# Building three of four blocks of gated one-hot rows for the first four groups inside the experts' stage

## The reference, cut to what matters

```
N, T, D = (4, 512, 128); NUM_EXPERTS = 8; k = int(EXPERT_CAP * t / NUM_EXPERTS)
probs = softmax(einsum('ntd,de->nte', x, gate_w)); probs = transpose(probs, (0, 2, 1))
g, m = top_k(probs, k)                              # gains and chosen tokens
xin = vmap(lambda xb, mb: xb[mb])(x, m)
h = gelu(einsum('nekd,edf->nekf', xin, w1)); h = einsum('nekf,efd->nekd', h, w2)
weighted = g[..., None] * h
out = zeros((n * t, d)).at[flat_idx].add(weighted)  # flat_idx: the chosen tokens
x = x + layernorm(out as bfloat16)
```

## Time and profile before

| | us |
|---|---|
| Median of 3 runs | 3795.21 |
| Lowest and highest run | 3792.87, 3801.27 |
| The profiled execution's own time | 3797.36 |
| Its span, first to last instruction | 3795.6 |
| Its mean granted TensorE clock | 0.868 |
| TensorE busy | 2975.8 (78%) |
| VectorE busy | 2390.8 (63%) |
| ScalarE busy | 1816.6 (48%) |
| GpSimd busy | 516.4 (14%) |

### The profile page before, as it was taken

The page is one execution under the profiler, slowest core; times in us unless marked ns, Lnnn a source line. Parts: engine busy times, 40 slices in busy tenths (PEclk is TensorE's granted clock), DMA queues, the critical chain, the costliest instruction groups (busy, mean ns, idle before and its releaser), DMA issues.

```text
span 3795.6 us, 76097 instructions
## 1 busy us (share of the span) xinstructions
PE 2975.8 (78%) x31950; PEld 2354.3 (62%) x31950; DVE 2390.8 (63%) x6446; ACT 1816.6 (48%) x3876; POOL 516.4 (14%) x643
## 2 busy tenths in 40 slices
PE   6788887778888758778884887967778798686885
PEld 3466665456666547667774765856666486574564
DVE  4655555565554578888897666467565845755337
ACT  3556555555555467777773443324434332343222
POOL 1110001120100132222222011120010202002000
PEclk7889988888998879898997988987989899697887
DMA  2000000000000010000000000000000000001000
GB/s 86 1 1 1 1 1 1 1 1 1 1 1 1 1 51 6 7 9 6 7 1 12 2 2 1 2 1 2 2 1 3 1 2 1 1 3 45 1 1 23
DMA packets 13542, 27.99 MB, mean 7 GB/s; under 512 B 784, under 2 KB 9232, under 8 KB 12688
## 3 DMA queue, kind: packets, MB, share of 16 engines
q1 hardware_dynamic: 13200, 23.12, 1.8%
HBM read 21.02 MB, written 2.10 MB: 6 GB/s over the span
## 4 chain that ended last, share of the span: by engine, by line
PE 50%; DVE 36%; ACT 10%; issue 3%; POOL 1%; DMA 0%; SPq 0%; DVEq 0%; POOLq 0%; ACTq 0%
PE ps L331 6%; DVE LN L1944 5%; PE ps L322 4%; PE ps L1822 3%; PE ps L1303 3%; DVE RS L237 3%; PE ps L388 3%; PE ps L296 3%; PE ps L475 3%; DVE M L491 2%; DVE LN L1957 2%; ACT LN L268 2%; PE ps L1314 2%; DVE LN L258 2%; PE ps L1766 1%
## 5 line engine op out<-in xcount | busy, mean ns | idle before, releaser
L304 ACT COPY LN<-ps 128x512 f32<-128x512 f32 (+4 forms) x592 | 303.3, 546 | 629.4 <-PE ps L296 172.2
L283 POOL TENSOR_TENSOR RS<-RS,MISC 128x4 f32<-128x4 f32 x216 | 219.2, 1015 | 2177.2 <-DVE RS L249 1642.6
L296 PE MATMUL ps<-cons,LN 128*128 128x128 f32 x672 | 143.2, 356 | 349.7 <-DVE LN L256 124.8
L296 PEld LDWEIGHTS ps<-cons,LN 128*128 128x128 f32 x672 | 97.8, 178 | 403.7 <-DVE LN L256 143.9
L491 DVE TENSOR_REDUCE M<-ps 128x6 f32<-128x768 f32 x256 | 242.0, 955 | 140.1 <-PE ps L475 95.7
L1944 DVE TENSOR_TENSOR LN<-LN 128x1024 f32<-128x1024 f32 (+2 forms) x192 | 220.3, 1147 | 27.8 <-ACT LN L304 16.9
L388 PE MATMUL ps<-LN 32*128 32x256 f32 x1024 | 187.4, 440 | 53.3 <-DVE LN L527 32.1
L632 DVE TENSOR_REDUCE M<-ps 128x12 f32<-128x1536 f32 x64 | 112.4, 1756 | 175.2 <-PE ps L378 175.2
L322 PE MATMUL ps<-LN,wAB 128*128 128x512 f32 x384 | 207.1, 672 | 14.3 <-ACT LN L341 8.5
L1822 PE MATMUL ps<-LN,wAB 128*128 128x128 f32 x1024 | 150.9, 310 | 74.3 <-ACT LN L304 73.8
L391 PE MATMUL ps<-LN 32*128 32x256 f32 x1024 | 202.9, 475 | 0.8 <-DVE M L491 0.8
(11 more groups left out here) (345 smaller groups left out, 7563.3 us busy)
## 6 DMA issues: line engine op xcount, KB each, us to landing
wAB<-wb SPq DMA_DIRECT2D x16, 256.0 KB, 2.7
LN<-wd SPq DMA_DIRECT2D x8, 512.0 KB, 6.9
wAB<-wa SPq DMA_DIRECT2D x1, 3840.0 KB, 16.1
wCs<-wc SPq DMA_DIRECT2D x1, 2336.0 KB, 10.7
XA<-xin SPq DMA_DIRECT2D x8, 256.0 KB, 7.6
y<-XA SPq DMA_DIRECT2D x8, 256.0 KB, 2.3
wAB<-wb SPq DMA_DIRECT2D x1, 1024.0 KB, 5.0
wAB<-wm SPq DMA_DIRECT2D x1, 1024.0 KB, 4.8
```

The lines of the kernel that those rows point to most:

```text
L283: pool.e.tensor_tensor(c.r[:, 40:44], c.r[:, 36:40], mhalf, ALU.pow).then_inc(*c.G.inc((k, "rstd")))
L296: ins = pe.e.transpose(ps[:, n * 128:(n + 1) * 128], src[:, n, :], ident)
L304: act.e.copy(dst, ps).then_inc(*c.A.inc(named(k, done)))
```

## The change

The eight instructions of a block, with their waits, become a function `dve_gated`. `dve_expert` calls it for the blocks (0, 0), (0, 1) and (1, 1) of the lane's first group: each ahead of the copy of one of the lane's first three items. `dve_put` then builds for the first four groups only block (1, 0). For groups 4 to 7 it builds all four as before. So that three blocks of a group can exist at once, block (1, 1) of group q < 4 lies in the token tiles of group q + 4; block (1, 0) still shares a buffer with (0, 0) and waits for its transposes. A block built in the experts' stage waits for the take stage of all sixteen sequences.

```diff
+        def gated_rows(q, m):
+            z = q + 4 if m and q < 4 else q
+            return [LN[:, 30720 + 512 * (q % 4):31232 + 512 * (q % 4)], LN[:, 16384 + 512 * z:16896 + 512 * z]]
...
             for it in range(n, 16, 4):
                 ex, hf = it // 2, it % 2
                 yield
+                if it < 12:
+                    dve_gated(dve, c, n, *((0, 0), (0, 1), (1, 1))[it // 4])
                 yield
                 dve_copy(dve, c, ("ex", it), YS[:, ex, 4 * hf:4 * hf + 4, :], v4(c.ps[0]), "sum", "y")
                 yield
+
+        def dve_gated(dve, c, q, m, eh):
+            if q < 4 and (m, eh) != (1, 0):
+                for b in range(16):
+                    dve.wait_ge(PD[b % 4], (("take", b), "taken", 1))
+            elif q < 4:
+                dve.wait_ge(c.P, (("put", q), 0, 0, "og_tr"))
+            elif m == 0:
+                dve.wait_ge(c.P, (("put", q - 4), 1, eh, "og_tr"))
+            else:
+                dve.wait_ge(c.P, (("put", q), 0, eh, "og_tr"))
+            g4 = gated_rows(q, m)[eh].rearrange("p (e b s) -> p e b s", e=4, b=2)
+            for e_ in range(4):
+                for b2 in range(2):
+                    cc = 8 * (2 * q + b2) + 4 * eh + e_
+                    ins = dve.e.tensor_scalar(g4[:, e_, b2, :], iota, RK[:, m, cc:cc + 1], GM[:, m, cc:cc + 1],
+                                              ALU.is_equal, ALU.mult)
+            ins.then_inc(*c.D.inc((("put", q), m, eh, "og")))
...
                 for m in range(2):
                     for eh in range(2):
-                        if m:
-                            dve.wait_ge(c.P, (k, 0, eh, "og_tr"))
...
-                        ins.then_inc(*c.D.inc((k, m, eh, "og")))
+                        if q >= 4 or (m, eh) == (1, 0):
+                            dve_gated(dve, c, q, m, eh)
                         yield
```

More of the change, by code:

```diff
@@ L2164, in pe_put @@
                 k = ("put", q)
-                og = [LN[:, 30720 + 512 * n:31232 + 512 * n], LN[:, 16384 + 512 * q:16896 + 512 * q]]
                 for m in range(2):
+                    og = gated_rows(q, m)
                     for eh in range(2):
```

## The result

The change takes 3775.43 us (median of 6 runs, 3769.0 to 3778.56) against 3794.04 us before (6 runs beside them, 3785.36 to 3801.39). The ratio is 0.9949, 95% interval 0.9932 to 0.9965: 18.6 us less. In a second comparison, six runs beside eleven of before, the ratio was 0.9943 (0.9925 to 0.9961).

The account below looks back on a forecast made before the run. TensorE bounds the experts' stage, then VectorE's block building bounds the start of the put stage and stays on the chain. 13.4 + 1.5 + 3.6 = 18.5 us won, 3795.21 - 18.5 = 3776.7, rounded to 3777; range 3770 to 3785.

Parts of the forecast that it names:

- later products: Put stage, products of groups 4 and 7: another clock could give 2.2 and 1.7 us or lose 0.6; taken as 0.
- step 3: Put stage, first and second reciprocal: one block instead of two stands ahead of each, 1.785 us twice, 3.6 us won.
- Step 1: Start of the put stage: fewer blocks ahead, seven sets of transposes then bound it; first product 13.4 us earlier.
- Step 2: Put stage, first product: clock stays up through the transposes, so it takes 3.84 us instead of 5.35, 1.5 us won.
- rival A: Start of the put stage: the clock falls all the same; only 13.0 us won, 3782 us; chance 0.12.
- Rival B: Put stage behind the cast: square root waits for something else, 14.9 us won, 3780, or 3785 with ScalarE's copies; chance 0.10.
- Cover in the experts' stage: Experts' stage: moved blocks fit VectorE's idle time, 4.60 us at the shortest against 1.785, leaving 2.8; cost 0.
- Rival C: Experts' stage: blocks make copies late, TensorE stops and the clock may drop; slower, up to 3809 us; chance 0.03.
- Rival D: Experts' or put stage: a wait holds VectorE or (1, 0) comes too late; no gain, 3795 us; chance 0.05.

Follow-up runs that it names:

- experiment with two blocks: Against the change, two blocks of each of the first four groups moved instead of three, (1,1) back in the put stage: 3771.39 us, ratio 0.9964 to before.
- that with four: Against the change, all four blocks of the first four groups built in the experts' stage, (1,0) in its own columns: 3765.08 us (one run).
- the one that was made late: Against the change, each of the twelve moved blocks built five times, four times into unused columns: 3793.76 us (one run), experts' stage 134.8 us.

## Why the prediction was right

The forecast of 3777 with 18.5 us won stands against 3775.43 and 18.6. By its steps, positions in the tail of the first profiles:

| step | predicted gain | measured |
|---|---|---|
| 1. start of the first product | 13.4 | 19.69 - 5.84 = 13.9 |
| 2. first product's length | 1.5 | 5.42 - 3.84 = 1.6 |
| first cast | 14.9 | 27.61 - 12.17 = 15.4 |
| 3. first and second reciprocal | 3.6 | 2.2 + 1.8 = 4.0 |
| second reciprocal | 18.5 | 47.89 - 28.42 = 19.5 |
| later products | 0 (up to 3.9) | 21.2 - 19.5 = 1.7 |
| experts' stage | 0 | 0.0 |

The second profiles agree on the start (13.9) and on step 3 (4.0). Their first product took 6.18 us before and 3.84 after, 2.3 less, so the second reciprocal came 20.2 us earlier, and the rest gave back 0.9.

**Step 1** was right in mechanism; seven sets of transposes took 3.28 us and not 3.6. The experiment with two blocks moves the product by the blocks put back, and that with four by the one taken away.

**Step 2** and rival A: the rows of 32 transposes were read rightly. That the clock of 0.50 in the earlier trace rows belonged to sparse transposes, not to transposes as such, is now shown from both sides, warm and cold.

**Step 3** was 0.4 too small. The set behind the remaining block of group 3 runs at the full clock, 0.64 us against 1.10; the prediction had named the change of clock for the products only. At the third reciprocal, where the order is the old one, the same 0.46 us was lost again, since the clock now stood low there. The set ahead of it, before and in the change:

```profile
3731.68 0.64 PE ps L2171 x4
```

```profile
3704.99 1.10 PE ps L2176 x4
```

Rival B falls by the experiment with two blocks: with the block back, cast to reciprocal is 10.0 us again. It was close: with the last block gone too, the square root waits for TensorE, only 1.8 us earlier.

**The later products** The earlier trace rows were given 0, with 2.2 and 1.7 as the kind case. They came to 6.12 - 5.30 = 0.8 and 5.47 - 3.84 = 1.6, the latter in part off the chain. The second profile of before had 4.91 and 3.84 for the same products, from where the change loses 0.4 and wins nothing. 0 lies between the 1.7 won and the 0.9 lost in the two pairs of profiles.

**Cover in the experts' stage**: 2.8 us to spare in the tightest place was the right number (2.81), and doubled work still fitted. Rival C is real only at more than double the price.

**Rival D** falls with the stage's unchanged length and the positions above.

The agreement of the total to 0.1 us is luck: its interval is 13 to 26 us. The tail, 19.3 to 21.2, is the sharper number, and the forecast was 1 to 3 us under it.

## What to carry to other kernels

Ask of a stage that is bound by one engine what the others will owe in the next one, and whether it depends on anything but old data: here VectorE idled for 100 us ahead of a stage in which it was the bound, and all that kept the work out was buffers. Look for those in dead columns; the first twelve blocks, 21.4 us of VectorE's work, took 21.2 us off the tail, and all 32, 57.1 us of work, took 60.4, since what stood behind a block on the chain shortened too. Judge small changes by the stretch of the trace that they touch, from a fixed event to the end, when whole executions differ by as much as the change is worth.

## What was not expected of the hardware

- Transposes count for the clock. After a gap at 0.50 they ran alone, without a pause: the clock was 0.50 from 3686.7 to 3689.8 and 1.00 from 3689.9 on. At 1.00, 100 of them kept it there for 10.7 us. The same transposes with gaps, 40 in 17 us, ran at 0.50 throughout.
- The same instructions ahead of the experts' stage took 3547.7 to 3569.5 us over twelve profiles, while the experts' stage took 113.49 or 113.50 us in all but the one that was made late. The tail repeated to 0.01 us in the two changed kernels that were profiled twice, and to 1.9 us in the kernel before.
